# Four transformer blocks on one core: the order of attention units between two batches, and row maxima taken for two heads at a time

## What is computed

```python
q, k, v = heads(h @ wq), heads(ctx @ wk), heads(ctx @ wv)     # blocks 0, 2: 64 wide; blocks 1, 3: 8 wide
q, k = rope(q), rope(k)                                       # block 0 only
sim = einsum('bhnd,bhmd->bhnm', q, k) * scale
a = softmax(sim, axis=-1)                                     # 256 queries, 256 or 1601 keys
x = x + einsum('bhnm,bhmd->bhnd', a, v).merge() @ wo + bo
```

## Time and profile before

| | |
|---|---|
| median of 3 runs | 6196.47 us (6185.82 to 6211.56) |
| profiled execution | 6242.82 us |
| its span, first to last instruction | 6241.0 us |
| busy: TensorE, VectorE, ScalarE, GpSimd | 91%, 70%, 54%, 40% of the span |

### The profile page before, as it was taken

The page is one execution under the profiler, slowest core; times in us unless marked ns, Lnnn a source line. Parts: engine busy times, 40 slices in busy tenths (PEclk is TensorE's granted clock), DMA queues, the critical chain, the costliest instruction groups (busy, mean ns, idle before and its releaser), DMA issues. The chain is left out here.

```text
span 6241.0 us, 170025 instructions
## 1 busy us (share of the span) xinstructions
PE 5692.5 (91%) x66584; PEld 3349.0 (54%) x66584; DVE 4360.4 (70%) x8986; ACT 3383.1 (54%) x7674; POOL 2505.9 (40%) x2223
## 2 busy tenths in 40 slices
PE   6999899988899989998889998999888998899988
PEld 4566346643556635664356653566435665356633
DVE  6886666656788666665788867666668886666664
ACT  3455565546544556554644556555564555655555
POOL 2566016730256501673026640277103663037700
PEclk9999699987899969998899987999779998699976
DMA  4000010000100001000010000100001000010000
GB/s 111 23 16 17 13 30 16 13 20 12 44 23 16 15 15 32 14 14 18 16 44 22 16 18 12 32 13 15 19 17 45 13 16 17 11 36 13 7 17 8
DMA packets 277771, 135.56 MB, mean 22 GB/s; under 512 B 151005, under 2 KB 266301, under 8 KB 276862
## 3 DMA queue, kind: packets, MB, share of 16 engines
q1 hardware_dynamic: 276990, 124.68, 8.5%
HBM read 101.90 MB, written 3.01 MB: 17 GB/s over the span
## 5 line engine op out<-in xcount | busy, mean ns | idle before, releaser
L2266 DVE TENSOR_REDUCE max_part<-ring 128x1 f32<-128x400 f32 (+2 forms) x4608 | 2418.6, 578 | 776.1 <-PE ring L1425 768.0
L1918 ACT ACTIVATE probs<-ring 128x512 f32<-128x512 f32 (+1 forms) x4096 | 2101.2, 572 | 1337.9 <-PE ring L1425 1312.4
L1401 POOL TENSOR_TENSOR weight_sum<-weight_sum,probs 128x512 f32<-128x512 f32 (+1 forms) x1408 | 1793.7, 1274 | 150.3 <-ACT probs L1918 11.5
L1425 PE MATMUL o_acc<-probs,region 128*32 128x256 f32 (+2 forms) x13312 | 1503.1, 441 | 47.2 <-ACT probs L1918 41.4
L1425 PEld LDWEIGHTS o_acc<-probs,region 128*32 128x32 f32 (+2 forms) x13312 | 617.2, 133 | 573.8 <-issue 262.4
L1401 POOL TENSOR_TENSOR weight_sum<-probs 128x512 f32<-128x512 f32 x256 | 332.1, 1297 | 1467.7 <-PE ring L1425 923.6
L1425 PE MATMUL ring<-qop,region 64*128 64x256 f16 x9984 | 833.1, 270 | 22.6 <-ACT shift_q L1763 16.7
L1763 ACT ACTIVATE region<-ring 65x128 f32<-65x128 f32 (+4 forms) x1232 | 560.9, 474 | 413.8 <-PE ring L1425 319.8
L1425 PE MATMUL ring<-nk,nq 32*128 32x400 f16 (+2 forms) x2560 | 601.9, 401 | 65.2 <-ACT probs L1918 51.1
L1425 PEld LDWEIGHTS ring<-qop,region 64*128 64x128 f16 x9984 | 522.2, 95 | 188.2 <-issue 92.1
L1425 PE MATMUL ring<-shift_q,shift_k 64*128 64x256 f16 (+1 forms) x3840 | 618.3, 270 | 0.0
(11 more groups left out here) (181 smaller groups left out, 6668.6 us busy)
## 6 DMA issues: line engine op xcount, KB each, us to landing
stage<-in_wide SPq DMA_DIRECT2D x448, 64.0 KB, 1.9
nk<-region SPq DMA_DIRECT2D x768, 25.0 KB
wo_stage<-in_wide SPq DMA_DIRECT2D x32, 512.0 KB, 4.0
stage<-in_wide SPq DMA_DIRECT2D x64, 128.0 KB, 2.5
v_stage<-in_wide SPq DMA_DIRECT2D x128, 64.0 KB, 1.9
ff_w<-in_ff_w SPq DMA_DIRECT2D x24, 256.0 KB, 3.3
stage<-kv_split SPq DMA_DIRECT2D x64, 96.0 KB, 2.1
v_stage<-kv_split SPq DMA_DIRECT2D x128, 48.0 KB, 1.7
```

The lines of the kernel that those rows point to most:

```text
L1401: pool.tensor_tensor(total, before, probs[0:rows_, (un.chunk + k) % PROBS, :], ALU.add)\
L1425: return pe.matmul(out, lhs, rhs, start=start, stop=stop, skip_group_check=True)
L1918: act.activation(to, src, ACT.Exp, scale=t.scale).then_inc(exp_done.sem, 1)
L2266: dve.tensor_reduce(dst, src, AX.X, ALU.max).then_inc(*release(one))
```

## The change

- The units are ordered by `make_items` in 17 phases. Even batches and odd batches are two streams, one stage pair apart: in a phase one batch runs wide self and wide cross, the other narrow self and narrow cross (the first phase has only a wide side, the last only a narrow one). The self units of the one stand before those of the other; in the cross part the 8 wide (X) and 4 narrow (x) units alternate by the string `SHARED`, and "+" places the narrow batch's passage to its next wide stage.
- A "max" job covers two heads: two matmuls into two neighbouring banks, one reduction over both. `Plan` picks neighbours for it, and other items take banks with few free neighbours. `RING` is 6.
- In wide cross units the query operand is made after the keys, and all maxima follow it.
- Rope: cosine and sine products both go to SBUF (`raw`, two slots; `raw_sin`, one), the sum, the high copy and the low part read SBUF; new waits guard the slots.
- Narrow values (`x_nv`, now of one batch) and narrow keys (`x_nk`) get buffers of their own outside `region`; the ones and zeros of `x_nv` are set once at the start and not on POOL in each narrow cross stage. `NK_SLOTS` falls from 3 to 2. Narrow outputs go to `attn_n` and wide ones to `attn`; maxima have two slots for each kind.
- The raw turns of the context move from stage 1 to stage 0; feed-forward weights are fetched for every batch. Waits and due times refer to the earlier unit of the same kind, and not to the earlier unit.

```diff
-POOL_BANKS, RING, SLOTS, PROBS = 7, 4, 4, 8
+POOL_BANKS, RING, SLOTS, PROBS = 7, 6, 4, 8
...
-NK_SLOTS, VS_SLOTS = 3, 4
+NK_SLOTS, VS_SLOTS = 2, 4
...
+        self.op_order = [*range(1, self.ops), 0] if cross else [*range(self.ops)]
...
-            return op(0) + op(1) + [("low", 0, 0), ("low", 1, 0), ("max", (0, None), 0), ("max", (1, None), 0),
-                                    ("shift", 0, 0)] + vals + end
+            return op(0) + op(1) + [("low", 0, 0), ("low", 1, 0), ("max", (0, None), 0), ("shift", 0, 0)] + vals + end
         def maxima(k):
-            return [("max", (h, q), k) for q in range(QT) for h in range(2)]
-
-        out = op(0) + op(1) + [("low", 0, 0)] + op(2) + [("low", 1, 0)]
-        out += op(3) + [("low", 2, 0)] + maxima(0) + op(4) + [("low", 3, 0)] + maxima(1)
-        out += vals[0:1] + [("low", 4, 0)] + maxima(2) + vals[1:2] + maxima(3)
+            return [("max", (0, q), k) for q in range(QT)]
+
+        out = op(1) + op(2) + [("low", 1, 0)] + op(3) + [("low", 2, 0)] + vals[0:1]
+        out += op(4) + [("low", 3, 0)] + op(0) + [("low", 4, 0), ("low", 0, 0)]
+        out += maxima(0) + maxima(1) + vals[1:2] + maxima(2) + maxima(3)
...
-            return [("spread", 0, 0), ("spread", 1, 0)] + [("max", (h, None), 0) for h in range(4)] + [("shift", 0, 0)]
-        out = [("max", (h, q), k) for q in range(QT) for k in range(len(self.kc)) for h in range(4)]
+            return [("spread", 0, 0), ("spread", 1, 0)] + [("max", (h, None), 0) for h in (0, 2)] + [("shift", 0, 0)]
+        out = [("max", (h, q), k) for q in range(QT) for k in range(len(self.kc)) for h in (0, 2)]
...
-        return [("load", 0, 0), ("stats", 0, 0), ("ln", 0, 0)]
+        return [("load", 0, 0), ("stats", 0, 0), ("ln", 0, 0)] + [("ctx", 0, j) for j in range(4)]
     out = []
+    if s == 1:
+        out += [("ctx", s, j) for j in range(4, 8)] + [("gate", s, 0)]
...
+STAGES = ((0, 1), (3, 4), (6, 7), (9, 10))
+SHARED = "XXxXxXXxXx+XX"
+
+
+def make_items():
+
+    out = [("pre", 0, 0)]
+    steps = len(STAGES) * B // 2
+
+    def unit(s, u, p):
+        out.append(("unit", s, u, p))
+
+    for phase in range(steps + 1):
+        wide = narrow = None
+        for side in range(2):
+            i = phase - side
+            if 0 <= i < steps:
+                u, k = 2 * (i // len(STAGES)) + side, i % len(STAGES)
+                if k % 2:
+                    narrow = u, *STAGES[k], k
+                else:
+                    wide = u, *STAGES[k]
+        if narrow:
+            out.append(("pre", narrow[1], narrow[0]))
+        if wide:
+            for p in range(ATT[wide[1]].units):
+                unit(wide[1], wide[0], p)
+            out.append(("pre", wide[2], wide[0]))
+        if narrow:
+            for p in range(ATT[narrow[1]].units):
+                unit(narrow[1], narrow[0], p)
+            out.append(("pre", narrow[2], narrow[0]))
+        at = {"X": 0, "x": 0}
+        for what in SHARED:
+            if what == "X" and wide:
+                unit(wide[2], wide[0], at[what])
+            elif what == "x" and narrow:
+                unit(narrow[2], narrow[0], at[what])
+            elif what == "+" and not narrow:
+                out.append(("pre", 0, 1))
+            elif what == "+":
+                u, k = narrow[0], narrow[3]
+                if k + 1 < len(STAGES):
+                    out.append(("pre", STAGES[k + 1][0], u))
+                else:
+                    out.append(("pre", END, u))
+                    if u + 2 < B:
+                        out.append(("pre", 0, u + 2))
+            if what != "+":
+                at[what] += 1
...
+            if what[0] == "scores" or is_max(what):
                 return 2
             return int(what[0] in ("pre", "job"))
+
+        def beside(r):
+            return sum(k in banks for k in (r - 1, r + 1))
+
+        def side_by_side():
+            return [r for r in banks if r + 1 in banks]
+
+        def pick(what):
+
+            if is_max(what):
+                r = min(side_by_side(), key=lambda r: beside(r) + beside(r + 1))
+                found = [r, r + 1]
+            else:
+                found = sorted(banks, key=beside)[:takes(what)]
+            for r in found:
+                banks.remove(r)
+            return found
...
-        x_v = region[:, X_KOP:X_WIDE].rearrange("p (z t c) -> p z t c", z=2, t=CT)
-        x_nv = region[:, 0:X_NV].rearrange("p (u t c) -> p u t c", u=2, t=CT)
-        x_nk = region[:, X_NV:X_NARROW].bitcast(F16).rearrange("p (s k) -> p s k", s=2)
+        x_v = region[:, X_KOP:X_COLS].rearrange("p (z t c) -> p z t c", z=2, t=CT)
...
+        x_nv = sb("x_nv", [P, CT, V_COLS])
+        x_nk = sb("x_nk", [P, 2, MP], F16)
...
-        ff_in = per_prelude("ff_in", lambda s, u: 32 * (u % 2 == 0 and s - 1 in FFN))
+        ff_in = per_prelude("ff_in", lambda s, u: 32 * (s - 1 in FFN))
...
+                    if kind == "max":
+                        h0, q = i
+                        a0, w = t.kc[k]
+                        for m, qq in enumerate(range(QT) if q is None else [q]):
+                            for h in range(2):
+                                part = slice(64 * h, 64 * h + 64)
+                                last = mm(ring[:, bank(one) + h, m * w:(m + 1) * w], qop[part, z, 0, qq * P:(qq + 1) * P],
+                                          kop_of(un)[part, 0, a0:a0 + w], True, True)
...
-                    copy(high, ring[:, bank(one), 0:w]).then_inc(op_high.sem, 1)
+                    copy(high, raw[:, raw_slot(un, i), 0:w] if t.rope else ring[:, bank(one), 0:w]).then_inc(op_high.sem, 1)
...
+                    if t.rope:
+                        dve.tensor_tensor(operand(un, i, 1)[0], raw[:, raw_slot(un, i), 0:w], high, ALU.subtract)\
+                            .then_inc(rope_low.sem, 1)
+                        return
...
-                    products, v = raw[:, i % 2, 0:w], ring[:, bank(one), 0:w]
-                    dve.wait_ge(*full(one))
+                    made = ("job", n, j)
+                    turned, v = raw[:, raw_slot(un, i), 0:w], ring[:, bank(made), 0:w]
+                    if one[0] == "sin":
+                        dve.wait_ge(*full(made))
+                        old = rope_before(un, i, 1)
+                        if old:
+
+                            dve.wait_ge(rope_step.sem, rope_step.at(old[0].n, old[0].t.rank(old[1]) + 1))
+                        dve.tensor_tensor(raw_sin[:, 0:w], v, rope_sin[:, a0:a0 + w], ALU.mult)\
+                            .then_inc(*release(made))
+                        return
                     if k == 0:
-                        dve.wait_ge(rope_step.sem, rope_step.at(n, 3 * max(i - 1, 0)))
-                        dve.tensor_tensor(products, v, rope_cos[:, a0:a0 + w], ALU.mult).then_inc(*release(one))
+                        dve.wait_ge(*full(one))
+                        old = rope_before(un, i, 2)
+                        if old:
+
+                            dve.wait_ge(rope_low.sem, rope_low.at(old[0].n, old[0].t.rank(old[1]) + 1))
+                        dve.tensor_tensor(turned, v, rope_cos[:, a0:a0 + w], ALU.mult).then_inc(*release(one))
                         return
-                    dve.tensor_tensor(v, v, rope_sin[:, a0:a0 + w], ALU.mult).then_inc(rope_step.sem, 1)
-                    dve.wait_ge(*taken(("job", n, j - 1)))
-                    dve.wait_ge(rope_step.sem, rope_step.at(n, 3 * i + 1))
-                    dve.tensor_tensor(v, v, products, ALU.add).then_inc(rope_step.sem, 2)
+                    for product in latest([("job", n, j - 1), made]):
+                        dve.wait_ge(*taken(product))
+                    dve.tensor_tensor(turned, turned, raw_sin[:, 0:w], ALU.add).then_inc(rope_step.sem, 1)
...
+                        both = ring[:, bank(one):bank(one) + 2, :]
                         if q is None:
-                            src = ring[:, bank(one), 0:QT * w].rearrange("p (q k) -> p q k", q=QT)
-                            dst = max_part[:, n % 2, 2 * h:2 * h + 2, 0]
+                            src = both[:, :, 0:QT * w].rearrange("p h (q k) -> p h q k", q=QT)
+                            dst = max_part[:, max_slot(un), 2 * h:2 * h + 4, 0].rearrange("p (h q) -> p h q", q=QT)
                         else:
-                            src, dst = ring[:, bank(one), 0:w], max_part[:, n % 2, 2 * h + q, k:k + 1]
+                            src, dst = both[:, :, 0:w], max_part[:, max_slot(un), 2 * h + q:2 * h + q + 3:2, k]
```

438 lines of the change are left out of this document (222 added, 216 removed).

## The result

The changed kernel takes **5941.6 us** in the median of four runs (5934.5 to 5970.2) against 6192.9 us of four runs of the kernel before beside it: a ratio of 0.960, 95% interval 0.957 to 0.963. That is 4.0% less time, 251 us, where the prediction had 13% and a range that ended at 5900. The profiled execution has a span of 5932.8 us and a mean granted clock of 0.955 (0.898 before).

The account below looks back on a forecast made before the run. TensorE bounds the wide cross stages; narrow ones lose to idling and half clock, 940 us over four rounds. Eight phases of each kind (8 x 667 = 5336) plus 122 gave 5458, 5400 us on the median's scale; range 5110 to 5900.

Parts of the forecast that it names:

- The sum: Whole kernel: eight phases with rope at 362 us, eight without at 305, plus 122 for the ends, 5458 us.
- How full TensorE stays: Mixed phases: full-clock TensorE work fills 93% of a phase with rope, 97% of one without.
- the prediction's last sentence: Rope phases: far above 362 us if VectorE, at 90%, delays maxima and with them scores; would make the forecast wrong.
- What TensorE has to do, at full clock: Busy time times clock by stage: 1290 of 1526 us a round; 343 us a phase with rope, 302 without.
- Maxima on TensorE: Two heads' products side by side: nothing to 0.17 us a pair, 24 a phase; a quarter taken, 6 us.
- Maxima on VectorE: 4608 reductions become 2304 of some 0.97 us; 0.08 us saved a pair, 11.5 us a phase, 184 in all.
- Rope through SBUF: Rope additions and low parts on VectorE: zero taken, bounds -8 to +200 ns on each of 896 instructions.
- The ends: Start 39 us, last narrow phase 43, first transition and last feed-forward 20 each without cover; together 122 us.
- two slots hidden: Narrow key slots, 3 to 2: 8 to 10 us of transfers hidden behind wide units of 20 us and more.
- Rival 1: Clock stays low in narrow work wherever it stands, 97 us a round remain: 5790 us; chance 0.08.
- Rival 2: TensorE waits for pairs of PSUM banks: 6710 us, slower (0.07); mild, 0.1 to 0.3 us a pair, 5630 to 6090 (0.10).
- Rival 3: Streams don't really overlap, only transitions gain, at most half of TensorE's 122 us idle a round: 5950 us; chance 0.05.

Follow-up runs that it names:

- experiment 3: Changed kernel with rope in the PSUM bank and single maxima, leaving the new order, buffers and six ring banks: 6238.1 us, ratio 1.005 to the kernel before.
- experiment 1: Changed kernel with the rope turned in the PSUM bank again, order, buffers and paired maxima kept: 5965.6 us, ratio 0.960 to the kernel before.
- experiment 5: Kernel before, old order and rope in the bank, with paired maxima and five ring banks in place of four: 6374.7 us, ratio 1.031.
- experiment 4: Changed kernel with `SHARED` reordered to six wide cross units, then four narrow ones in a group: 6497.3 us, ratio 1.046 to the kernel before.
- experiment 9: Changed kernel with five banks of the ring in place of six: 6107.4 us, ratio 0.986 to the kernel before.
- experiment 11: Changed kernel with another alternation, `SHARED` = XxXXxXxXXx+XX, first narrow unit one place earlier: 6122.9 us, ratio 0.988 to the kernel before.
- experiment 10: Changed kernel with rope in the bank, three narrow key slots, one slot for rope products, four for narrow maxima: 5885.6 us, ratio 0.951 to the kernel before.
- experiment 6: Changed kernel with paired products on TensorE but two single-bank reductions on VectorE, banks released after the second: 5980.3 us, ratio 0.967 to the kernel before.

## Why the prediction was wrong

**The sum, split.** It had 4974 us for phases 1 to 15 (7 x 362 + 8 x 305) and 484 for the two outer phases and the ends. The trace has 5328.7 (5679.4 - 350.7) and 604 (350.7 + 253.4). Of the 475 us missed, 355 are in the mixed phases and 120 at the ends.

The prediction's own quantity splits it further: TensorE's busy time times the granted clock, taken piece by piece over the trace, is the work at full clock; the rest of the span is idle time and what the half clock costs. For whole profiled executions (us; the forecast on the same scale, 5458):

| | work at full clock | idle | lost to the half clock |
|---|---|---|---|
| kernel before | 5136 | 549 | 557 |
| order alone (experiment 3) | 5352 | 435 | 458 |
| order and pairs (experiment 1) | 5203 | 494 | 268 |
| the whole change | 5200 | 521 | 212 |
| pairs alone, old order (experiment 5) | 5008 | 733 | 636 |
| narrow units in a group (experiment 4) | 5070 | 773 | 653 |
| forecast of the whole change | 5064 | 394 together | |

**How full TensorE stays: the step that failed most.** I took shares of 0.93 and 0.97 of each phase as work at full clock, 0.950 over the fifteen. They were 0.905 and 0.942 in phases 9 and 10, and 0.910 over the fifteen: 350 us idle and 131 lost to the half clock, 481 where the sum had 247. So 234 of the 355 us are here. I had read the shares from TensorE's busy time in the wide stages (88 to 98%) and put the clock beside it at 1, although the wide self stage with rope stood at 0.93. The rope phases were the ones to fear by the prediction's last sentence, but they missed by no more than the others: 386 us in the mean against 362, and 328 against 305, with VectorE at 82% of phase 9 and 67% of phase 10. What keeps TensorE from staying full is only in part known. The runs show that it hangs on banks (166 us for the sixth, experiment 9), on the alternation (181, experiment 11) and on the buffers of the narrow units (experiment 10); of the idle time after the change, 122 us are waits for max_part.

**What TensorE has to do, at full clock: the second step that failed.** I took busy time times clock of each stage as work that moves with it into any order. It doesn't: with the order alone it rose by 216 us. In the old order a single wide maximum's product mostly stood beside another maximum or a score product of its own stage; the order took these neighbours away, and the products of the wide cross maxima rose from 251 to 388 us at full clock. The narrow maxima rose from 322 to 382, the narrow values and scores by 7 (683 to 690). The remaining 12 us are spread over the rest. So the order, which I had at some -680 us before the pairs (8 x 680 + 122 against 6242.8), brought 216 us more work and 213 us less of idle time and half clock, and was worth +144 with the old banks and +41 with the new ones. In phases 9 and 10 it did 349 and 314 us of work, where I had 343 and 302, and left 47 and 39 us idle or to the half clock, where my shares left 26 and 9. After the pairs, the mixed phases had 4848 us of work against the forecast's 4727: the other 121 of the 355.

**Maxima on TensorE: undersized.** I took a quarter of the bound, 6 us a phase, 96 in all, because in the earlier trace rows two of three stood together already. That was the old order. In the new one, the pairs gave 273 us without the detour and 381 with it, 17 and 24 a phase, VectorE's part included. TensorE's half alone gave 342 (experiment 6). Only a part of this is the term that I had: from experiment 3 to experiment 1 the work at full clock fell by 149 us, 9 a phase, while the loss to the half clock fell by 190 and the idle time rose by 60. A higher clock as a gain of the pairs stood nowhere in the sum, and why it came is not shown. For the wide maxima the two errors belong together: what the order parts (251 to 388 us), the pair brings together again (261). In the old order the pairs took 128 us of work as well, but idle time and half clock grew by 263.

**Maxima on VectorE: right.** 984 ns against 970. I had 184 us of VectorE's time; two reductions in place of one cost it 124 (4485.3 less 4361.4, experiment 6), and the time rose by 39, which is hardly clear of the noise (ratios 0.967 and 0.960).

**Rope through SBUF: wrong in price, right in the time.** I took zero within -8 to +200 ns an instruction. VectorE pays 174 us (experiment 1), at the upper bound of 179. It is a hold, not a slower instruction. Of the 192 additions of 400 columns after the change, the 135 that ran while GpSimd did nothing took 558 to 578 ns; the 35 that lay over GpSimd's work for nine tenths of their length or more took 1269 in the mean and up to 1675. Timeline of both engines in one such place:

```profile
287.37 2.84 POOL L1511 TENSOR_TENSOR weight_sum<-weight_sum,probs 128x512 f32<-128x512 f32 x2
288.01 1.07 DVE L2343 TENSOR_TENSOR region<-raw,region 128x400 f16<-128x400 f32 x1
289.00 1.64 DVE L2373 TENSOR_TENSOR raw<-raw,raw_sin 128x400 f32<-128x400 f32 x1
290.17 1.06 POOL L1519 TENSOR_TENSOR attn<-attn,o_inv 128x256 f32<-128x256 f32 x1
290.57 0.41 DVE L2369 TENSOR_TENSOR raw<-ring,rope_cos 128x256 f32<-128x256 f32 x1
```

The addition ends at 290.64, 0.43 us behind GpSimd's pair of instructions (290.21; GpSimd's spans are rough), where it takes 0.57 by itself; the product that reads the bank, 0.41 us, runs beside GpSimd's next instruction unhurt. The row on which I had settled, x_out at 425 ns, was taken while GpSimd was idle, and the centring at 498, which I called far, was the same hold: 342 ns free, 1214 over GpSimd's work (20 of them). The Trainium skill (SBUF — State Buffer, SBUF: two separate sides) states it: a VectorE instruction with two SBUF inputs and a GpSimd instruction that reads SBUF share a port pair under an exclusive lock, and the loser waits for the whole instruction. The trace agrees, by these numbers; the centring, with one tensor and two scalars per row, is held as well. Yet no time came of it: with pairs, 174 us of VectorE are worth nothing measurable (5942 and 5966). Without pairs the detour costs 84 us (6322 and 6238). That the banks, which it frees earlier and which pairs want (experiment 9), pay for it with pairs is an argument, not shown.

**The ends: undersized.** Phase 0 took 350.7 us and the last phase 230.2, where I had 142, half of a narrow self and cross stage before ((82.1 + 202.0)/2). Halving was wrong because the start of a stage doesn't halve: the first self unit ended 64.4 us behind phase 15 and the first cross unit 60.9 behind the self part, together 125 of the 230, with nothing of another batch over them. The self part took 79.4 us against 41, the cross part 150.8 at half clock against 101. The key slots come on top. I had called two slots hidden since two wide units lie between narrow ones. In the last phase none does; I had named that case, at up to 10 us a unit, and left it out of the sum. With a third slot, and the edits beside it, the three later cross units took 65 us in place of 90 (experiment 10).

**The rivals.** Rival 1 (half clock stays) is refuted: 0.97 over the fifteen mixed phases. Rival 2 is there in the waits (TensorE on max_part 122 us, 32 before), but 90 us over 2304 pairs are 0.04 us each, under its mild form of 0.1 to 0.3; in the old order the pairs did turn out slower, by 3% (experiment 5). Rival 3, with 5950, came nearest in time and is wrong in mechanism: narrow and wide units do alternate, and when they don't the clock falls (experiment 4).

## What to carry to other kernels

Busy time times clock is not work that can be moved as it stands. Here a wide maximum's product cost 0.11 us beside a neighbour in other rows and 0.29 without, so before a reordering count which matmuls on part of the rows have a neighbour within a few ns, and ask who it will be after. Nor does a busy share carry over: put a price on the idle time and the clock of the mixture each by itself, and don't take the clock as full where the rows don't have it so. What starts a stage isn't halved when a stage is. Two changes of which one cost 3% alone and the other brought nothing made 4% together; price parts in the order in which they enable one another. And here a VectorE instruction moved from PSUM to SBUF had a second price wherever GpSimd worked beside it.

## What the runs showed of the hardware

- An addition, a subtraction or a centring on VectorE with all operands in SBUF took 569, 573 and 342 ns (the last of 128 columns, before the change) with GpSimd idle, and 1269, 1468 and 1214 in the mean where nine tenths of it or more lay over GpSimd's instructions; with one operand in PSUM the means were 554 to 583 ns at 400 columns in either case.
- Two matmuls of a wide pair on different rows started 3 ns apart in the median. From start to start, counted up to its own duration, a narrow maximum's product cost 0.125 us in pairs and 0.192 where a third had no neighbour (phase 9, after and experiment 3).
- The half clock didn't cost all narrow products alike. In the kernel before, by the same count, the narrow values took 0.062 us at full clock and 0.117 at half, the score products 0.063 and 0.092, the maxima's products of 400 columns 0.152 and 0.223.
- The order alone had a clock of 0.93 in phases 9 and 10, the whole change 0.97 and 0.99, at a busy share of TensorE that was no higher (95 and 96%, then 93 and 95%).
